# Key-value products of two batches in one run, in a block of three attentions on one core

## The reference

```python
k = (encoder_seq @ Wk.T + bk).reshape(B, T_enc, 16, 32)
v = (encoder_seq @ Wv.T + bv).reshape(B, T_enc, 16, 32)
kv = jnp.einsum('bthd,bthe->bhde', k, v)
att = jnp.einsum('bqhd,bhde->bqhe', q, kv) * scale
return layer_norm(att + decoder_seq, ln_gamma, ln_beta)
```

## Time and profile before

| | us |
|---|---|
| runs shown | 580.87, 575.29, 579.4 |
| median | 579.4 |
| profiled execution | 576.12 |
| its span | 574.4 |
| round of the loop | 34.04 |

### The profile page before, as it was taken

How to read it: one execution, slowest core, us unless ns; L and a number is a source line. 1 busy time by engine, 2 the same in 40 slices (tenths; PEclk the granted TensorE clock), 3 DMA queues, 4 the chain that set the end, 5 groups by cost and what they waited for, 6 DMA issues and landing times.

```text
span 574.4 us, 11752 instructions
## 1 busy us (share of the span) xinstructions
PE 567.4 (99%) x5017; PEld 485.3 (84%) x5019; DVE 347.8 (61%) x385; ACT 205.0 (36%) x296; POOL 229.3 (40%) x182
## 2 busy tenths in 40 slices
PE   9999999999999999999999999999999999999997
PEld 7889899898988989888678898978888888888886
DVE  4887963655627356562588557566676347767741
ACT  4444352504435151442472352423251122435220
POOL 2599786573727557264424100202435443000000
PEclk9999999999999999999999999999999999999999
DMA  8464424231322422204240410105922222799501
GB/s 310 139 220 156 147 85 155 74 112 49 141 82 73 155 73 75 81 1 141 76 148 3 157 68 11 73 2 136 229 86 111 109 73 74 176 226 243 161 1 73
DMA packets 24757, 64.72 MB, mean 113 GB/s; under 512 B 2409, under 2 KB 2409, under 8 KB 21777
## 3 DMA queue, kind: packets, MB, share of 16 engines
q1 hardware_dynamic: 24720, 64.18, 35.3%
HBM read 63.00 MB, written 1.18 MB: 112 GB/s over the span
## 4 chain that ended last, share of the span: by engine, by line
PE 85%; DVE 4%; ACT 2%; issue 1%; DMA 1%; POOL 0%; DVEq 0%
PE ps L333 18%; PE ps L335 17%; PE ps L334 17%; PE ps L858 8%; PE ps L881 3%; PE ps L885 3%; PE ps L873 2%; PE ps L868 2%; PE ps L867 2%; PE ps L872 2%; PE ps L935 1%; PE ps L1179 1%; PE ps L899 1%; DVE lo L1423 1%; DMA raw<-in_ctx 1%
## 5 line engine op out<-in xcount | busy, mean ns | idle before, releaser
L472 POOL TENSOR_TENSOR psum_tmp<-psum_tmp,raw 128x512 f32<-128x512 f32 (+1 forms) x88 | 146.8, 1668 | 28.7 <-DVE lo L1423 20.0
L858 PE MATMUL ps<-hi 128*128 128x256 f32 (+3 forms) x416 | 129.6, 313 | 0.8 <-DVE lo L1423 0.8
L1423 DVE TENSOR_TENSOR lo<-raw,hi 128x2048 fp32r<-128x2048 f32 (+1 forms) x29 | 63.3, 2199 | 30.1 <-ACT hi L541 30.1
L858 PEld LDWEIGHTS ps<-hi 128*128 128x128 f32 (+1 forms) x416 | 78.7, 189 | 1.9 <-DVE lo L1423 1.1
L333 PE MATMUL ps<-hi,gh 128*128 128x512 f32 x192 | 75.5, 393 | 0.0
L335 PE MATMUL ps<-hi,gl 128*128 128x512 f32 x192 | 74.8, 390 | 0.0
L334 PE MATMUL ps<-lo,gh 128*128 128x512 f32 x192 | 74.7, 389 | 0.0
L522 POOL TENSOR_TENSOR sx<-sx,raw 128x512 f32<-128x512 f32 x32 | 41.1, 1291 | 78.2 <-DVE raw L1764 78.1
L745 ACT ACTIVATE hi<-raw 128x2048 fp32r<-128x2048 f32 x14 | 26.8, 1918 | 87.0 <-PE ps L335 76.8
L333 PE MATMUL ps<-wvh,gh 128*128 128x512 f32 x128 | 51.1, 399 | 0.2 <-DVE gl L1575 0.2
L335 PE MATMUL ps<-wvh,gl 128*128 128x512 f32 x128 | 50.0, 391 | 0.0
(11 more groups left out here) (229 smaller groups left out, 1177.9 us busy)
## 6 DMA issues: line engine op xcount, KB each, us to landing
raw<-in_ctx SPq DMA_DIRECT2D x23, 1024.0 KB, 4.8
raw<-in_ve SPq DMA_DIRECT2D x8, 1024.0 KB, 5.2
raw<-in_oe SPq DMA_DIRECT2D x8, 1024.0 KB, 7.2
wk<-gm_rows SPq DMA_DIRECT2D x8, 512.0 KB, 9.9
g<-gm_rows SPq DMA_DIRECT2D x8, 512.0 KB, 10.7
raw<-in_ctx SPq DMA_DIRECT2D x8, 130.0 KB
xres<-in_x SPq DMA_DIRECT2D x1, 1024.0 KB, 9.7
mb<-in_WqT SPq DMA_DIRECT2D x1, 1024.0 KB, 13.6
```

What stands on the lines that cost most here:

```text
L472: pool.tensor_tensor(psum_tmp[0:k, :], (raw[:, 0, :] if t == 1 else psum_tmp[0:k, :]), raw[0:k, t, :], ALU.add).then_inc(ctx_sum, 1)
L858: pe.matmul(dst, hi[0:kk, t, cols], x, start=start and opens, stop=stop and closes, skip_group_check=True)
L1423: dve.tensor_tensor(lo[0:k, r, :], raw[0:k, r, :], hi[0:k, r, :].bitcast(F32), ALU.subtract).then_inc(ctx_lo, 1)
```

## The change

The loops on TensorE, ScalarE and VectorE take two batches in a round (b = 2 and 4), and batch 6 stands unrolled behind them. M of an odd batch is copied to another place, `mb_odd`: columns 128 to 383 of all eight `kv[:, b]`, which nothing else uses in the loop. So M of two batches lives at the same time, and `kv_pair(b)` makes the products of the batches b and b + 1 in one run of 128, into columns 0 to 127 and 128 to 255 of bank 6. It stands at the ends 2 to 3, 4 to 5 and 6 to 7. The ends 1 to 2, 3 to 4 and 5 to 6 have no such products any more, and the split behind the loop is gone. The wait of `m_part` for `kv_done` stands only in the rounds behind a pair. VectorE copies both results out one behind the other (`kv_keep_pair`).

```diff
+        mb_odd = kv[:, :, :].rearrange("p (k s) n -> p k s n", s=2)[:, :, :, P:3 * P]
+        mb_even = mb[:, :, :].rearrange("p k (s n) -> p k s n", s=2)
...
-            def m_copy(b, ms=range(KC)):
+            def m_copy(b, ms=range(KC), into=mb_even):
                 for m in ms:
                     act.wait_ge(m_mm, b * 4 + m + 1)
-                    act.activation(mb[:, m, :], bank[6 + m % 2][:, :], ACT.Copy).then_inc(m_done, 1)
+                    act.activation(into[:, m, :, :], bank[6 + m % 2][:, :].rearrange("p (s n) -> p s n", s=2), ACT.Copy).then_inc(m_done, 1)
...
+            with act.Fori(2, B - 2, 2) as b:
+                round_of(b, mb_odd)
+                round_of(b + 1, mb_even)
+            round_of(B - 2, mb_odd)
...
-                if not first and m == 0:
+                if kept and m == 0:
                     pe.wait_ge(kv_done, b)
...
+            def kv_products(m_rows, at):
+
+                for c in range(KC):
                     for k in range(KC):
                         for j in range(4):
-                            cols = slice(c * P + D1 * j, c * P + D1 * j + D1)
-                            mm = pe.matmul(head_block(bank[6], c, j), wk[:, k, cols], mb[:, k, cols],
-                                           start=(k == 0), stop=(k == KC - 1))
+                            first = D1 * (c % 2 * 4 + j)
+                            mm = pe.matmul(head_block(at, c, j), wk[:, k, c * P + D1 * j:c * P + D1 * j + D1],
+                                           m_rows[:, k, c // 2, first:first + D1], start=(k == 0), stop=(k == KC - 1), skip_group_check=True)
+                return mm
...
+            def kv_pair(b):
+
+                pe.wait_ge(m_done, b * 4 + 8)
+                kv_products(mb_even, bank[6][:, 0:P])
+                kv_products(mb_odd, bank[6][:, P:2 * P]).then_inc(kv_mm, 2)
...
-            with pe.Fori(2, B - 1) as b:
-                kv_part(b - 2)
+            def round_of(b, kept):
                 gram(b, False)
-                products_of(b - 1, False, lambda: mirror(b), lambda: g_transposes(b))
-            kv_part(B - 3, range(0, 2))
-            gram(B - 1, False, lambda: kv_part(B - 3, range(2, KC)))
+                products_of(b - 1, False, kept, lambda: mirror(b), lambda: g_transposes(b))
+
+            with pe.Fori(2, B - 2, 2) as b:
+                round_of(b, False)
+                kv_pair(b - 2)
+                round_of(b + 1, True)
+            round_of(B - 2, False)
+            kv_pair(B - 4)
+            gram(B - 1, False)
...
-            def kv_keep(b):
-                dve.wait_ge(kv_mm, b + 1)
+            def kv_keep_pair(b):
+                dve.wait_ge(kv_mm, b + 2)
                 dve.tensor_copy(kv[:, b, 0:P], bank[6][:, 0:P]).then_inc(kv_done, 1)
+                dve.tensor_copy(kv[:, b + 1, 0:P], bank[6][:, P:2 * P]).then_inc(kv_done, 1)
...
+            with dve.Fori(2, B - 2, 2) as b:
+                round_of(b)
+                kv_keep_pair(b - 2)
+                round_of(b + 1)
+            round_of(B - 2)
+            kv_keep_pair(B - 4)
```

More of the change, by code:

```diff
@@ L613, in _, with round_of @@
             gh_high(1)
-            with act.Fori(2, B - 1) as b:
+            def round_of(b, into):
                 for c in range(1, 4):
@@ L618, in _ @@
                 ctx_high(b + 1, 0, False)
-                m_copy(b - 1)
+                m_copy(b - 1, into=into)
                 gh_high(b)
+            with act.Fori(2, B - 2, 2) as b:
+                round_of(b, mb_odd)
+                round_of(b + 1, mb_even)
+            round_of(B - 2, mb_odd)
             for c in range(1, 4):
@@ L907, in g_transposes, with m_part @@
                 mm.then_inc(gt_mm, 1)
-            def m_part(b, m, first):
+            def m_part(b, m, first, kept=True):
                 if first and m == 0:
@@ L925, in m_part, with kv_part @@
                 mm.then_inc(m_mm, 1)
[L927 to L931, removed]
+            def kv_products(m_rows, at):
+                for c in range(KC):
                     for k in range(KC):
                         for j in range(4):
-                            cols = slice(c * P + D1 * j, c * P + D1 * j + D1)
-                            mm = pe.matmul(head_block(bank[6], c, j), wk[:, k, cols], mb[:, k, cols],
-                                           start=(k == 0), stop=(k == KC - 1))
-                if cs.stop == KC:
-                    mm.then_inc(kv_mm, 1)
+                            first = D1 * (c % 2 * 4 + j)
+                            mm = pe.matmul(head_block(at, c, j), wk[:, k, c * P + D1 * j:c * P + D1 * j + D1],
+                                           m_rows[:, k, c // 2, first:first + D1], start=(k == 0), stop=(k == KC - 1), skip_group_check=True)
+                return mm
+            def kv_part(b):
+                pe.wait_ge(m_done, b * 4 + 4)
+                kv_products(mb_even, bank[6][:, 0:P]).then_inc(kv_mm, 1)
+            def kv_pair(b):
+                pe.wait_ge(m_done, b * 4 + 8)
+                kv_products(mb_even, bank[6][:, 0:P])
+                kv_products(mb_odd, bank[6][:, P:2 * P]).then_inc(kv_mm, 2)
             def last_kv_part():
@@ L957, in last_kv_part, with products_of @@
                 mm.then_inc(kv_mm, 1)
-            def products_of(b, first, halfway, between):
-                m_part(b, 0, first)
+            def products_of(b, first, kept, halfway, between):
+                m_part(b, 0, first, kept)
                 m_part(b, 1, first)
@@ L981, in _ @@
             gram(1, False)
-            products_of(0, True, lambda: mirror(1), lambda: g_transposes(1))
-            with pe.Fori(2, B - 1) as b:
-                kv_part(b - 2)
+            products_of(0, True, False, lambda: mirror(1), lambda: g_transposes(1))
+            def round_of(b, kept):
                 gram(b, False)
-                products_of(b - 1, False, lambda: mirror(b), lambda: g_transposes(b))
-            kv_part(B - 3, range(0, 2))
-            gram(B - 1, False, lambda: kv_part(B - 3, range(2, KC)))
+                products_of(b - 1, False, kept, lambda: mirror(b), lambda: g_transposes(b))
[6 more added lines that the diff above has]
+            gram(B - 1, False)
             def row_sums():
@@ L1524, in _, with round_of @@
             gl_lower(1)
-            kv_keep(0)
-            with dve.Fori(2, B - 1) as b:
+            def round_of(b):
                 ctx_low(b, 1)
@@ L1535, in _ @@
                 gl_lower(b)
-                kv_keep(b - 1)
+            with dve.Fori(2, B - 2, 2) as b:
[4 more added lines that the diff above has]
+            kv_keep_pair(B - 4)
             ctx_low(B - 1, 1)
```

## The result

The changed kernel takes 590.9 us (median of 587.45, 590.76, 590.98, 593.7), the kernel before 578.1 beside it (575.29 to 580.87); the ratio is 1.022, with an interval of 1.014 to 1.030. It is slower by 2.2%, where I had forecast 581.2 us and no change that can be told. The profiled execution took 587.45 us with a span of 585.7, 11.3 more than the span before.

What follows compares the result with a forecast made beforehand. TensorE, busy 99% of the 574.4 us span, was taken to bound the kernel. Terms of -0.69, +2.12 and +0.40 summed to +1.8 us, on the median 579.4 giving 581.2 us; range 575.3 to 584.4.

Steps and rivals of the forecast that it cites:

- Term 1: Three round ends losing their run: L881 still waits for VectorE's remainder, so 0.23 us gained each, -0.69 us together.
- The rival of no hold: Ends without a run: L881 doesn't wait, three ends gain 1.46 us each; -1.9 us in all, 577.5 us; chance 0.10.
- Term 2: Ends 2 to 3 and 4 to 5: a run of 128 products takes 2.29 us, 1.06 more each, +2.12 us.
- Term 3: Last end, 6 to 7: split run 6.25 us, one unsplit run 5.59, double run 6.65; +0.40 us.
- Parts 4 and 5: Copies into the odd place counted at nothing; VectorE's paired copies out of the bank hidden with about 0.8 us to spare.
- Part 6: Removed kv_done waits were long fulfilled; longer loop bodies change one TensorE jump in four, and a jump shows no cost.
- The long run that loses pace: Second half of three double runs slower: +3.5 us, 582.9; over 1% slower from 2.4 us per added half; chance 0.04.
- The rival of the clock: Three 1.2 us holds at L881 lower the clock to 1.2 GHz; 1% needs 1.3 us lost per hold; chance 0.04.

Runs made afterwards that it cites:

- the doubled run: Kernel before with each 64-product run inside TensorE's loop, and by oversight batch 6's full run behind it, made twice: 594.87 us against 579.67.
- the other operands: Changed kernel with the second half of each double run reading mb again instead of the odd place in kv: 590.49 us against 579.67.
- the kernel with the inner loop: Changed kernel, double run as two passes over the same 64 products from mb: 581.31 us against 579.67, then median 585.3 against 576.4.

## Why the prediction was wrong

**Term 1, the ends without a run: right.** -0.13, -0.23 and -0.27 us for a forecast of -0.23 each; the holds of 1.24, 1.22 and 1.22 us are there. The rival of no hold has fallen. What it would have brought was too high, though: with the hold taken away the chunk behind is the next limit in the first round.

**Term 2, the double runs: this step failed.** I took the pace of runs of 32 and 64 products and drew it out to 128. The array does keep that pace, 2.29 us where the code has been passed before. But a run in fresh code needs its instructions as fast as it uses them, two for each record and 128 records in 1.1 us. The rows that I used could not show this, since in the kernel before no run was longer than 128 records, and a block is just that long. The step was "from below this can't be under 1.06 at this pace; from above ... 1.63": the upper bound was the pace of products of another shape and not a limit of supply. (The rows of other long runs left out two of the very same shape, lines 783 and 950, which take 1.2 us for 128 records; they would have given the same pace and, with 128 records each, no sign of the stop either.) In place of 1.06 each the added halves cost 4.4 us at the first double run (1.06 and 3.35), 1.06 at the second and 3.2 at the third (1.06 and 2.13), 8.7 for the 3.2 in my sum; in another execution the first cost 9.1 (43.19 us for the stretch, at half clock in part).

**Term 3: right,** by the kernel without the split (22.29 for 22.93), once the stop of 2.13 us is set apart.

**Parts 4 and 5: right.** The copies into the odd place take 0.60 us as before, and VectorE's pair of copies hid at the second double run (184.34 to 184.83) as it should.

**Part 6, the code: this step failed too.** I looked at the jumps of the loop and saw that they cost nothing, and from that I took the whole question of code to be closed. Not the jump was the place but straight code that is passed once. The profile of before had a sign: the queue named "instruction" on its page, with 29 packets, none of them between 110 and 245 us. The prediction doesn't mention it. The third double run stands behind the loop, in code that is passed once; that it would have run through inside the loop is argued from the second, not shown.

**The rivals.** The long run that loses pace had the right place, the second half of the double runs, and the right sign. It had a wrong mechanism (a stop, not a pace), so its price, 2.4 us for each added half, was passed in the first and the third (4.4 and 3.2) and not at all in the second; I had given it 0.04 because its price came from a row of another shape. The rival of the clock was right that it falls, wrong about where: not behind the holds of 1.2 us at the ends without a run, behind none of which a profile shows a fall, but at the double run and at the distances, from 338.9 us on. What its fall hangs on is only partly shown. In the profiles, the clock fell in each of the six executions with a stop of 3.7 to 4.1 us in the first double run, between 2.4 us into the stop and 1.2 us behind it (at 113.2 to 115.5 us), and in none of the four with a stop of 3.35 or less there. It also fell in the stop of 5.29 us of the doubled run. But no length of the stop divides them: at the third double run it fell in a stop of 2.44 us, in the kernel without the hold, and not at one of 2.67, with the other operands. The second place, where it fell between 330 and 347 us in five profiles, has stops of 1 to 3 us of its own in most of them, with and without the lower clock; one of the five is the kernel before with its run in one piece. And the clock falls in executions of the kernel before as well, less often. Why a block comes ahead in one execution and late in the next stays open, and so does what part of a stop is the load's beside it.

The Trainium skill has the mechanism, and I had not drawn on it. Runtime: NRT & Kernel Launch, section Instruction fetch mechanics, says that instructions are fetched in blocks of 16 KiB, 256 instructions, by a queue of the engine's own. The 128 records between two stops, each a load and a product, agree with this. It also says that this fetch is mostly hidden, as issuing is slower than filling. In wide products this case agrees: the kernel before takes 29 packets, and no wait put down to "issue" in it is longer than 0.84 us. In runs of small products it doesn't hold: a stop at a boundary took 1.7 to 5.3 us there, and 0.8 to 1.3 with a tile between.

## What to carry to other kernels

Count the instructions of a run of tiny products, not only its array time: where a run is longer than a block of code (here 128 records of load and product, 1.1 us), it can stop for 2 to 5 us in code that is passed for the first time. Wide products in the middle of it shortened the stops here, and where a loop came back to it there was none. Merging such runs to save waits of 0.3 us can so cost ten times what it saves. When an end of one stage is covered by other work, compare the chain beside it first: here taking away 1.5 us of work gained 0.2.

## What the runs showed of the hardware

A stop for code moves with the code, to the record, when 64 small products are put in 100 us earlier. From the packet of instructions to the next weight load it was 2.3 to 3.0 us in all 22 stops. The stops of one program differ between executions (one of 3.35 us, or two of 4.03 and 1.77, in the first double run), and its times spread more: 587 to 598 us for the changed kernel, 574 to 582 for the one before. So one execution can mislead: the kernel with the inner loop was 1.6 us above before in its first and 9 us in the median of four others.
